# Attention and NF4 feed-forward layer on one core: zero rows by DMA, turns spread over more steps, high parts subtracted in PSUM

## The reference

```python
# x: 4 x 512 x 512, 32 heads of 16; w1, w2: 1376 x 512, w3: 512 x 1376
q, k, v = (x @ w.T + b for each of (wq, bq), (wk, bk), (wv, bv))     # reshaped to (B, S, H, D)
scores  = einsum('bshd,bstd->bsht', q, k) / sqrt(16)   # for every token: 32 heads against 32 heads
context = einsum('bsht,bstd->bshd', softmax(scores), v)
x  = layernorm(x + context)
dq = nf4_quant_dequant(w)      # w1, w2, w3: blocks of 64, absmax scaling, nearest of 16 levels
h  = silu(x @ dq1.T) * (x @ dq2.T)
out = layernorm(x + h @ dq3.T)
```

## Time and profile before

| | us |
|---|---|
| runs of the kernel | 797.81 median of 3 (794.51, 797.81, 806.0) |
| the profiled execution, its own time | 802.0 |
| its span, first to last instruction | 800.2 |
| PE busy | 731.4 (91%) |
| DVE busy | 648.1 (81%) |
| ACT busy | 475.7 (59%) |
| POOL busy | 116.8 (15%) |
| mean granted TensorE clock | 0.851 |

### The profile page before, as it was taken

One profiled execution on the slowest core, in us unless ns is written; L12 is line 12 of the kernel. 1 busy time (PEld: TensorE's weight loads), 2 busy tenths in 40 slices (PEclk: granted clock), 3 DMA queues, 4 the chain that ended last, 5 costly groups with the idle time before them and its releaser, 6 DMA issues.

```text
span 800.2 us, 14244 instructions
## 1 busy us (share of the span) xinstructions
PE 731.4 (91%) x5668; PEld 624.6 (78%) x5668; DVE 648.1 (81%) x896; ACT 475.7 (59%) x629; POOL 116.8 (15%) x95
## 2 busy tenths in 40 slices
PE   4899999937989999999899989898999999999983
PEld 4778788837989999998677868787888888788761
DVE  2799999999897997986569699999897586765386
ACT  3688989855645636455546577676664456642124
POOL 2011104242101111010102021121111010100022
PEclk9999999975555655555899999999999999999995
DMA  9965445899957995947203631201414101250347
GB/s 223 228 165 162 147 148 171 216 295 242 245 126 182 253 256 151 282 123 269 100 1 135 210 133 53 81 27 55 122 66 158 48 2 34 74 195 12 115 149 157
DMA packets 89330, 116.22 MB, mean 145 GB/s; under 512 B 24720, under 2 KB 70800, under 8 KB 86448
## 3 DMA queue, kind: packets, MB, share of 16 engines
q1 hardware_dynamic: 88128, 113.21, 50.2%
q10 hardware_dynamic: 1136, 2.10, 1.2%
HBM read 76.42 MB, written 38.86 MB: 144 GB/s over the span
## 4 chain that ended last, share of the span: by engine, by line
PE 49%; DVE 23%; issue 10%; ACT 8%; DMA 6%; SPq 2%; POOL 2%; DVEq 0%; POOLq 0%; ACTq 0%
DVE nf_acc L1079 11%; PE ps_p L960 10%; PE ps_s L879 6%; PE ps_s L878 6%; PE ps_s L877 6%; ACT nf_y L724 5%; PE ps_p L877 5%; PE ps_p L879 5%; PE ps_p L878 5%; PE ps_s L947 3%; PE ps_t L898 2%; DMA qk_parts<-qk_p 2%; DMA dequantised<-nf_acc 2%; DVE nf_acc L1075 1%; PE ps_t L902 1%
## 5 line engine op out<-in xcount | busy, mean ns | idle before, releaser
L1079 DVE SCALAR_TENSOR_TENSOR nf_acc<-nf_y,nf_acc 128x1024 f32<-128x1024 f32 (+4 forms) x266 | 306.5, 1152 | 31.6 <-ACT nf_y L724 22.0
L724 ACT ACTIVATE nf_y<-nf_w,bound_b 128x1024 f32<-128x1024 f32 (+4 forms) x285 | 289.7, 1048 | 21.0 <-DVE nf_acc L1079 10.7
L960 PE MATMUL ps_p<-probT,v_bd 128*68 128x32 f32 x1024 | 125.5, 302 | 4.5 <-DVE probT L1128 4.5
L960 PEld LDWEIGHTS ps_p<-probT,v_bd 128*68 128x68 f32 x1024 | 122.7, 211 | 5.8 <-issue 3.2
L643 POOL TENSOR_TENSOR nf_w<-nf_w,nf_rec 128x1024 f32<-128x1024 f32 (+4 forms) x19 | 38.9, 2048 | 346.3 <-DVE nf_rec L1063 346.3
L1234 DVE TENSOR_TENSOR silu<-silu,ps_s 128x512 f32<-128x512 f32 (+1 forms) x44 | 30.1, 684 | 71.5 <-PE ps_s L879 71.4
L877 PE MATMUL ps_p<-x_hl,w_hl 128*128 128x512 f32 x192 | 77.5, 404 | 5.4 <-DVE w_hl L1097 3.4
L879 PE MATMUL ps_p<-x_hl,w_hl 128*128 128x512 f32 x192 | 75.8, 395 | 0.0
L877 PE MATMUL ps_s<-x_hl,f_ha 128*128 128x512 f32 x192 | 75.7, 394 | 0.0
L879 PE MATMUL ps_s<-x_hl,f_la 128*128 128x512 f32 x192 | 75.6, 394 | 0.0
L878 PE MATMUL ps_s<-x_hl,f_ha 128*128 128x512 f32 x192 | 75.5, 393 | 0.0
(11 more groups left out here) (100 smaller groups left out, 1259.2 us busy)
## 6 DMA issues: line engine op xcount, KB each, us to landing
x_hl<-x_parts SPq DMA_DIRECT2D x10, 2048.0 KB, 8.6
qk_parts<-qk_p SPq DMA_DIRECT2D x64, 204.0 KB, 2.5
q_st<-qk_parts SPq DMA_DIRECT2D x48, 272.0 KB, 6.6
k_st<-qk_parts SPq DMA_DIRECT2D x48, 272.0 KB, 7.5
x_parts<-x_st SPq DMA_DIRECT2D x16, 512.0 KB, 4.5
nf_w<-in_L_ffn_w SPq DMA_DIRECT2D x24, 256.0 KB, 3.2
dequantised<-nf_acc SPq DMA_DIRECT2D x10, 512.0 KB, 2.8
v_blocks<-v_t SPq DMA_DIRECT2D x16, 256.0 KB, 3.3
```

Of the source, the lines that this page charges most:

```text
L724: act.activation(nf_y[0:p, at % NY, 0:w], nf_w[0:p, u % 2, 0:w], ACT.Identity, bias=bound_b[0:p, i:i + 1], scale=STEEP).then_inc(s_ny, 1)
L960: t = pe.matmul(ps_p[0:MV, (G + 3) % NPV, i * H:(i + 1) * H], v_bd[hb % 2][:, :, g * GI + i], probT[:, G % 2, i], start=True, stop=True)
L1079: dve.scalar_tensor_tensor(out=acc, in0=y, scalar=float(NF4[i + 1]), in1=acc, op0=ALU.min, op1=ALU.max).then_inc(s_nacc, 1)
```

## The change

1. **Zero rows by DMA.** POOL no longer clears the stacks. Rows 3, 7, 11, ... of the first pair are copied by two DMAs out of `v_bd_0` while that is still zero, and those of the second pair out of the first pair. The ones of `v_bd_0` are written after that. `v_bd` is cleared in four pieces.
2. **The first load stands two tiles earlier** in SP's list (`FIRST_LOAD` 37 instead of 39), and the two DMAs of zeros stand ahead of it. For the second pair, two DMAs of zeros stand ahead of its 12 loads.
3. **Five levels move into the second seam** (`LV_T`), between the last groups of attention and the first FFN step, and the FFN table is flatter: 3 or 2 levels in the first five steps, 4 in steps 5 to 31, then 7, 7, 7, 7, 6, 6.
4. **Turns of the FFN's start are spread**: two in each of steps 0 and 1, the context turns in steps 2 to 4 (before, steps 0 and 1 had three each), and what follows one step later.
5. **Low parts of 20 turned FFN weights** (`LOW_A`): behind the down product TensorE multiplies the high part by a negated identity into the bank that still holds the turned piece (`rest`), and ScalarE copies what is left in it out as the low part at the start of its next step. VectorE does nothing for them.
6. The store semaphores are split by slot.

```diff
-    FIRST_LOAD = 3 * KC * (NBK - 1) + 3
+    FIRST_LOAD = 3 * KC * (NBK - 1) + 1
-    LV_F = [(1, 2)] * 4 + [(2, 2)] + [(1, 2)] * 2 + [(2, 3)] * 8 + [(2, 2)] * (FIRST_OF[2] - 15) + [(3, 3)] * 6
+    LV_T = (2, 3)
+    LV_F = [(1, 2)] * 2 + [(1, 1)] * 2 + [(1, 2)] + [(2, 2)] * (FIRST_OF[2] - 5) + [(3, 4)] * 4 + [(3, 3)] * 2
...
-    F_TURNS = {0: [("f", W_UNITS[2], 0), ("f", W_UNITS[2], 1), CT_LAST[0]],
-               1: [("f", W_UNITS[3], 0), ("f", W_UNITS[3], 1), CT_LAST[1]],
-               2: CT_LAST[2:4], 3: CT_LAST[4:], 5: XT_LAST[:2], 6: XT_LAST[2:]}
-    MOMENTS_F, NORM_F = 3, 4
+    F_TURNS = {0: [("f", W_UNITS[2], 0), ("f", W_UNITS[2], 1)], 1: [("f", W_UNITS[3], 0), ("f", W_UNITS[3], 1)],
+               2: CT_LAST[:2], 3: CT_LAST[2:4], 4: CT_LAST[4:], 6: XT_LAST[:2], 7: XT_LAST[2:]}
+    MOMENTS_F, NORM_F = 4, 5
...
+    LOW_A = {key: n for n, key in enumerate(k for s in range(8, NS) if s - 1 not in FIRST_OF
+                                       for k in F_TURNS.get(s, []) if k[0] == "f")}
...
+        def low_done(eng, key):
+            if key in LOW_A:
+                eng.wait_ge(s_ta, LOW_A[key] + 1)
+            else:
+                eng.wait_ge(s_tl, LOW_V[key] + 1)
...
                 if tau == FIRST_LOAD:
+                    sp.wait_ge(s_proj, 3 * KC * (NBK - 1))
+                    sp.wait_ge(s_vzero[0], Q4)
+                    for st in st_0:
+                        sp.dma_start(st[3::4].rearrange("r h t -> r (h t)"),
+                                     v_bd_0[3::4].rearrange("r m t -> r (m t)").bitcast(BF16)).then_inc(s_szero[0], 16)
                     parts_stored(sp, 2 * KC)
-                    sp.wait_ge(s_szero, 2)
                     load_stacks(sp, 0)
                     values_stored(sp, KC)
-                    sp.wait_ge(s_vzero, 1 + Q4)
+                    sp.wait_ge(s_vzero[0], 2 * Q4)
                     load_v(0)
-            sp.wait_ge(s_szero, 4)
+            sp.wait_ge(s_proj, 3 * KC * NBK)
+            sp.wait_ge(s_szero[0], 16 * 2)
+            for st, zero in zip(st_1, st_0):
+                sp.dma_start(st[3::4].rearrange("r h t -> r (h t)"), zero[3::4].rearrange("r h t -> r (h t)")
+                             ).then_inc(s_szero[1], 16)
             load_stacks(sp, 1)
...
+            levels(sum(LV_T))
             load_x1(0)
             load_x1(1)
...
-                pool.memset(v_bd[slot][:], 0.0).then_inc(s_vzero, 1)
...
-            def clear_stacks(slot):
...
-                for st in stacks[slot]:
-                    pool.memset(st[:].bitcast(F32), 0.0).then_inc(s_szero, 1)
+                    pool.memset(v_bd[slot][:, DV * q:DV * q + DV], 0.0).then_inc(s_vzero[slot], 1)
+
+            def ones(slot):
+
+                pool.wait_ge(s_vzero[slot], Q4)
+                for q in range(Q4):
+                    pool.memset(v_bd[slot][32 * q:32 * q + 32, DV * q + D], 1.0).then_inc(s_vzero[slot], 1)
...
+            def low(key):
+                act.wait_ge(s_rest, LOW_A[key] + 1)
+                src, dst = turn_shape(key)
+                act.activation(dst[1], src, ACT.Copy).then_inc(s_ta, 1)
...
             context(GG - 2)
+            steep(LV_T[0])
             for key in TAIL_2:
                 high(key)
             context(GG - 1)
-
+            steep(LV_T[1])
+
+            parts_stored(act, 2 * KC * NBK)
+            values_stored(act, KC * NBK)
+            act.wait_ge(s_ident, 2)
+            act.activation(minus_i[:], ident[:], ACT.Copy, scale=-1.0).then_inc(s_minus_i, 1)
             for s in range(NS):
                 n, j = STEPS[s]
                 rows = rows_of(j)
+                for key in F_TURNS.get(s - 1, []):
+                    if key in LOW_A:
+                        low(key)
                 act.wait_ge(s_gate, s + 1)
...
+            def rest(key):
+
+                pe.wait_ge(s_th, HIGH[key] + 1)
+                src, dst = turn_shape(key)
+                rows = src.shape[0]
+                pe.matmul(src, minus_i[0:rows, 0:rows], dst[0], start=False, stop=True,
+                          skip_group_check=True).then_inc(s_rest, 1)
...
                 if g == 0:
+                    pe.wait_ge(s_szero[hb % 2], 16 * 2)
...
+            pe.wait_ge(s_minus_i, 1)
             for s in range(NS):
                 gate_up(s)
                 for key in F_TURNS.get(s, []):
                     turn(key)
                 if s:
                     down(s - 1)
+                for key in F_TURNS.get(s, []):
+                    if key in LOW_A:
+                        rest(key)
...
-            for key in TAIL_1 + TAIL_2:
+            for key in TAIL_1:
                 low(key)
+            lift(LV_T[0])
+            for key in TAIL_2:
+                low(key)
+            lift(LV_T[1])
```

More of the change, by code:

```diff
@@ L195, in layer_kernel @@
         if g == 1:
-            back = max(back, 8 if kind == "t" else 4)
+            back = max(back, 9 if kind == "t" else 5)
         else:
@@ L286, in layer_kernel @@
         s_const = sem("s_const")
-        s_vzero = sem("s_vzero")
-        s_szero = sem("s_szero")
+        s_vzero = [sem(f"s_vzero{i}") for i in range(2)]
+        s_szero = [sem(f"s_szero{i}") for i in range(2)]
         s_pad = sem("s_pad")
@@ L295, in layer_kernel @@
         s_tl = sem("s_tl")
+        s_minus_i = sem("s_minus_i")
+        s_rest = sem("s_rest")
+        s_ta = sem("s_ta")
         s_proj = sem("s_proj")
@@ L330, in layer_kernel @@
         s_dq = sem("s_dq")
-        s_dst = sem("s_dst")
+        s_dst = [sem(f"s_dst{i}") for i in range(2)]
         s_rld = [sem(f"s_rld{u}") for u in range(NU)]
@@ L700, in _ @@
                 around(LV_A[G] - LV_A[G] // 2)
+            around(sum(LV_T))
             for s in range(NS):
@@ L882, in turn @@
                 n = TURN[key]
-                wait(pe, s_tl, n - 3 if n < NPT else n - 1)
+                if n >= NPT:
+                    low_done(pe, TURNS[n - 2])
+                elif n >= 4:
+                    low_done(pe, TURNS[n - 4])
                 kind, k, c = key
@@ L972, in gate_up @@
                     pe.wait_ge(s_th, HIGH[last] + 1)
-                    pe.wait_ge(s_tl, TURN[last] + 1)
+                    low_done(pe, last)
                 xx = x1_hl[b % 2]
@@ L1243, in _ @@
                         add_context(key)
-                    else:
+                    elif key not in LOW_A:
                         low(key)
```

63 lines of the change are left out of this document (32 added, 31 removed).

## The result

| | before | after |
|---|---|---|
| median of the runs, us | 798.38 (4 runs) | 811.90 (4 runs, 810.72 to 813.16) |
| ratio to before | | 1.0158, 95% interval 1.0081 to 1.0235 |
| the profiled execution: own time / span | 802.0 / 800.2 | 811.45 / 809.6 |
| mean granted TensorE clock | 0.851 | 0.847 |

The changed kernel is slower, by about 1.5%. The forecast was 800, the range 786 to 812: the time lies 0.1 us inside the range's upper end, which is luck. So most of what follows is about the 12 us that the forecast did not have, 10 of them in the FFN.

What follows compares the result with a forecast made beforehand. PE, busy 91% of the span, was taken as the bound, so only its idle time, half clock or work could be given back. 802.0 + 8.0 + 8.6 - 19.5 + 4.2 + 1.0 = 804.3, on the median's footing 800 us; range 786 to 812.

Steps and rivals of the forecast that it cites:

- The first seam: Projections into attention: ScalarE held at tile 30 until tile 25's store lands at 166.4; scores 4 at 202, +8 us.
- the slow-zeros rival: First seam: zero DMAs slower than loads, 13 us instead of 4.3 a pair, giving 817 us; chance 0.08.
- Attention behind it shifts as a whole: Attention after scores 4: the first seam's +8 us delay was to carry through it.
- The second seam: Attention into FFN: step 0 waits for input loads now behind levels, +6.9 us, and +1.7 for half clock: +8.6.
- The FFN: FFN steps: waits and clock losses in steps 0, 1, 9, 13 and 16 go, -19.5 us, against +4.2 and +1.0.
- that in step 16 (2.6) too, since unit 11 now has more room: -2.6: FFN step 16: PE's wait on the reloaded weight goes, -2.6 us.
- The price of `rest`: FFN: 20 extra matmuls on PE without cover where PE is full, +4.2 us, twice that if each changes operand.
- VectorE's relief in steps 7 to 16: FFN: fewer levels and no low parts, about 1.3 + 1.3 us less a step in steps 7 to 10, ending waits.
- The drain of step 33: FFN end: seven levels instead of six in step 32 lengthen a drain PE already waited on, +1.0 us.
- the footing: Whole kernel: the profiled execution before lay 4.2 us above the median, so 804.3 was restated as 800 us.

Runs made afterwards that it cites:

- e9: Changed kernel with first load at tile 39, input loads before seam levels, identity off seam, unit 11 turned in step 16, low parts on VectorE, POOL clearing both pairs: 0.9831.
- e11: The kernel of e10 with the low parts taken off VectorE again (subtraction by TensorE, copy by ScalarE): 792.57 us, 0.9869 of the kernel before.
- e2: Changed kernel with the FFN's input loaded ahead of the seam's unit load and the negated identity made at G = 16: 806.32 us, 1.0060 of before.
- e7: The kernel before with only the second pair's zeros by DMA instead of POOL: 802.53 us, 0.9992 of before.
- e3: Changed kernel with five levels instead of four in FFN steps 12 to 14, taken from the last steps, so unit 11 turns in step 16: 806.32 us, 1.0048.
- e4: Changed kernel with all low parts of turns back on VectorE, everything else as it is: 810.04 us, 1.0085 of the kernel before.
- e10: The kernel of e9, but second pair's zeros by DMA, five levels in FFN steps 9 to 13 and two in step 14: 789.93 us, 0.9852 of before.

## Why the prediction was right and wrong

**The first seam: right, mechanism and numbers.** ScalarE waited at tile 30 as forecast, and PE stood idle for 10.33 us in the projections until 167.24. L1132 came down to 2.38 us (predicted about 2.07). The store of tile 25 was to let ScalarE go at 166.4: 165.7. Scores 2 at 186.4: 185.61. Scores 4 at 202: 202.91. Both zeros had landed 6.1 us after the first was issued, where I had taken 4.3 us for the bytes and let a landing follow; the slow-zeros rival (13 us) is out. The Trainium skill (SBUF — State Buffer, Who interferes with whom) says that whoever issues first gets the shared port pair for the whole instruction. It doesn't say who gets it next: that L1075 would get in between two POOL instructions was my reading of it, and no run bears that out. With a scaling alone it took 2.05 to 2.45 us in all thirteen traces, and with a scaling and two memsets 9.77 us, twice, in two kernels (the earlier trace rows and e9).

**"Attention behind it shifts as a whole": wrong, by 2.9 us.** Of 8.8 us at scores 4, 5.9 remained. PE's wait of 3.12 us for ScalarE's context copy at G = 10 is gone. It stands in the two kernels in which VectorE has its stall (before, e9: 3.12 and 2.47 us) and in none of the eleven executions without it, whether their scores 4 start at 195.6 (e11) or at 206.2 (e2). So it was a late effect of the stall, which I had taken for hidden by the second pair's loads. That PE comes later is part of it but not all: in e11 scores 4 start 1.0 us later than in e9, and the copy still ends 0.5 us sooner (229.1 against 229.6). By which way it gets there (the levels that stand behind the stall in VectorE's list and ahead of the copies in ScalarE's) is in the main argued; the traces show that VectorE has idle time to catch up before scores 4 without the stall (4.72 us in e7, 3.75 in e11) and none with it. Part of what the missing wait gives is taken back: all eleven have PE standing 0.8 to 1.8 us in the middle of scores 7 ("issue"), which neither of the two has. Its cause is open.

**The second seam: right.** Predicted 6.9 us by SP's wait, plus 1.7 of clock; measured 6.1, and 2.6 of clock (2.8 us in the window behind the wait, less the 0.2 lost there before): 8.7 for 8.6. That the parts miss by 0.8 and 0.9 in opposite directions is luck. e2 made both edits and the wait was gone.

**The FFN: the step that failed** is "that in step 16 (2.6) too, since unit 11 now has more room: -2.6". It priced only what the later turn takes away, the wait on the reload. The turn moved from step 16 to step 17 and so stands directly ahead of down(16), the first product that reads it, with its low part on VectorE behind the drain of step 17. It cost 5.9 us of wait and 1.5 us of clock. Steps 16 and 17 were to take 2.6 us less than before and took 4.7 more; e3, which moves the turn back, takes 4.6 us off them. This is the greater part of the 10 us.

**The price of `rest`: mis-sized.** Predicted +4.2 (20 matmuls by 0.227 us), up to 8.4. By the steps that hold one it is 5.3 us, 1.1 more than forecast. The gain for which I had set it off, VectorE's relief in steps 7 to 16, did not come from it: e4 has no waits there without it. Four levels a step instead of five gave it, as e10 shows from the other side: with five, a drain of 4.60 us stands in step 13 again. Either would have done: with five levels and the low parts off VectorE it is 0.70 us (e11).

**The drain of step 33: right in sign, too small.** The wait rose from 1.55 to 2.35 us, near the +1.0 that I had, but the 1.7 us of clock behind it was not in the forecast: step 33 takes 2.4 us more than before. In the two executions of the changed kernel the clock fell there (0.57 over 4 us in both), and in e4, behind a longer wait, it did not; why is open. The drain of step 5 rose from 1.07 to 1.74 us, with the clock at 1.00 behind it; step 5 as a whole is no longer than before.

Against the forecast on the profiled executions' footing, 804.3, the changed kernel's own 811.45 is 7.2 us more: -2.1 from attention (5.9 for 8.0), -0.8 from the wait of the second seam, +10.1 from the FFN. Of these 10.1, by the lengths of the steps in the two traces against the forecast's terms for them, 7.3 lie in steps 16 and 17, 1.4 in step 33, and 1.4 in all the others, of which `rest` is 1.1. The other 4.7 us between 800 and 811.9 are the footing: I took 4.2 us off for an execution of before that lay above its median, and the changed kernel's profiled execution lies 0.45 below its own.

## What to carry to other kernels

A gap of PE is worth no more than what stands late behind it: ask for each wait removed which transfer or copy is due next and when, and what the means of removing it puts in a queue (e7: 6.7 us won at scores 2, none kept in the kernel's time). A turn, load or fill that a table lets slide by one step has to be laid beside the first instruction that reads it, in the lists of both the engines that make it, before its old wait is counted as a gain. Work moved to an engine that is 91% busy must buy waits at more than its own price, and where several edits move together the cheap ones (a table, an order of two loads) should be tried without the dear one.
